# One block instead of two, token sums behind weight pieces, an earlier reciprocal and two warm-up products fewer

## The reference

```python
xn = _layernorm(x)                            # over 512 channels
# attention: 32 query heads, 8 key/value heads, head size 128, window 128
q, k, v = xn @ wq, xn @ wk, xn @ wv
q, k = _rope(q, pos), _rope(k, pos)           # rotary embedding
scores = einsum('bqhgd,bshd->bhgqs', qg, k) * sm_scale     # causal, last 128 positions
s = softmax(scores) @ v @ wo
# feed-forward, inner width 1792, weights = (int - zero) * scale per 128 rows
g = silu(xn @ gate_proj) * (xn @ up_proj) @ down_proj
out = x + s * silu(g)
```

## Time and profile before

| what | value |
|---|---|
| three runs: median (lowest to highest) | 885.1 us (884.85 to 885.5) |
| the profiled execution: its own time | 885.35 us |
| its span, first to last instruction | 883.6 us |
| mean granted TensorE clock | 0.998 of full speed |
| DVE busy | 691.7 us (78%) |
| ACT busy | 485.5 us (55%) |
| POOL busy | 534.6 us (61%) |
| HBM traffic | 69 GB/s over the span |

### The profile page before, as it was taken

The page is one execution under the profiler, slowest core; times in us unless marked ns, Lnnn a source line. Parts: engine busy times, 40 slices in busy tenths (PEclk is TensorE's granted clock), DMA queues, the critical chain, the costliest instruction groups (busy, mean ns, idle before and its releaser), DMA issues. The chain is left out here.

```text
span 883.6 us, 14045 instructions
## 1 busy us (share of the span) xinstructions
PE 870.4 (99%) x4354; PEld 733.2 (83%) x4354; DVE 691.7 (78%) x1106; ACT 485.5 (55%) x1308; POOL 534.6 (61%) x430
## 2 busy tenths in 40 slices
PE   8999999999999999999999999999999999999997
PEld 7778888888888888888888888888877878888886
DVE  7887877877786877877786877877777888889876
ACT  4766556555656565565656565555663334444533
POOL 4675555555555555456555555554457898887865
PEclk9999999999999999999999999999999999999999
DMA  8011010110101011001101010003223464655632
GB/s 255 28 52 37 25 49 24 37 37 29 37 29 36 24 47 36 24 24 36 47 24 36 24 47 24 24 0 108 72 72 108 118 199 147 171 151 155 167 132 96
DMA packets 84596, 61.54 MB, mean 70 GB/s; under 512 B 3664, under 2 KB 71888, under 8 KB 84560
## 3 DMA queue, kind: packets, MB, share of 16 engines
q1 hardware_dynamic: 83840, 59.98, 23.4%
q10 hardware_dynamic: 720, 1.11, 0.3%
HBM read 58.98 MB, written 2.10 MB: 69 GB/s over the span
## 5 line engine op out<-in xcount | busy, mean ns | idle before, releaser
L1333 POOL TENSOR_TENSOR q_lo<-work,q_hi 128x512 fp32r<-128x512 f32 x64 | 82.9, 1295 | 157.8 <-ACT q_hi L1205 157.8
L36 PE MATMUL ps<-xt_hi,w_lo 128*128 128x512 f32 x444 | 175.1, 394 | 1.9 <-PEq L846 1.5
L37 PE MATMUL ps<-xt_lo,w_hi 128*128 128x512 f32 x444 | 173.4, 391 | 0.0
L38 PE MATMUL ps<-xt_hi,w_hi 128*128 128x512 f32 x444 | 173.2, 390 | 0.0
L1338 POOL TENSOR_TENSOR pt_lo<-kept,pt_hi 128x512 fp32r<-128x512 f32 x112 | 143.6, 1300 | 24.5 <-ACT pt_hi L1226 24.5
L1215 ACT ACTIVATE probs<-ps,neg_max 128x128 f32<-128x128 f32 x256 | 90.7, 367 | 53.3 <-DVE neg_max L1484 53.3
L1226 ACT ACTIVATE pt_hi<-kept 128x512 fp32r<-128x512 f32 x112 | 69.2, 633 | 65.7 <-DVE kept L1494 65.7
L36 PE MATMUL ps<-wo_hi,o_lo 128*128 (+1 forms) x256 | 99.8, 390 | 1.1 <-DVE o_lo L1500 1.0
L38 PE MATMUL ps<-wo_hi,o_hi 128*128 (+1 forms) x256 | 99.6, 389 | 0.0
L37 PE MATMUL ps<-wo_lo,o_hi 128*128 (+1 forms) x256 | 99.6, 389 | 0.0
L36 PEld LDWEIGHTS ps<-xt_hi,w_lo 128*128 128x128 f32 x444 | 83.7, 188 | 18.5 <-issue 2.4
(11 more groups left out here) (166 smaller groups left out, 2143.1 us busy)
## 6 DMA issues: line engine op xcount, KB each, us to landing
work<-L_attn_wq SPq DMA_DIRECT2D x32, 256.0 KB, 2.8
work<-L_attn_wo SPq DMA_DIRECT2D x32, 256.0 KB, 2.6
work<-L_ffn_gate_w SPq DMA_DIRECT2D x14, 256.0 KB, 3.4
work<-L_ffn_gate_z SPq DMA_DIRECT2D x14, 256.0 KB, 4.6
work<-L_ffn_gate_s SPq DMA_DIRECT2D x14, 256.0 KB, 5.7
work<-L_ffn_up_w SPq DMA_DIRECT2D x14, 256.0 KB, 3.2
work<-L_ffn_up_z SPq DMA_DIRECT2D x14, 256.0 KB, 3.9
work<-L_ffn_up_s SPq DMA_DIRECT2D x14, 256.0 KB, 4.4
```

Source lines behind the costliest of these rows:

```text
L36: pe.matmul(out, stat[1], mov[0], start=first, stop=False, skip_group_check=grown)
L37: pe.matmul(out, stat[0], mov[1], start=False, stop=False, skip_group_check=grown)
L38: return pe.matmul(out, stat[0], mov[0], start=False, stop=last, skip_group_check=grown)
L1333: pool.tensor_tensor(lo, row_of(unit, b, i), hi.bitcast(F32), ALU.subtract).then_inc(rope_split, 1)
```

## The change

1. Attention and FFN no longer open a block each. Both functions return five lists, and one block runs them one behind the other, so the barrier between is gone. ScalarE gets a wait for the last output projection (`y_ready`) ahead of its first FFN instruction; VectorE had one already.
2. In the last unit GpSimd makes the weight piece first and the x part behind it; `t24` moves from the last attention block to the head of the FFN list. Its `t_lo` parts of the first half stand between or behind the weight pieces 3, 4 and 5.
3. In the first unit, at j = 0 and j = 1, the reciprocal of the next block stands inside the first rotation, between the sine and the cosine products; ScalarE scales before it splits that rotation's result.
4. In the first seven-product block ScalarE's third `copy` stands ahead of the first split of sums for the next block.
5. 22 idle products instead of 24.

```diff
@@ ffn_block, low_parts (GpSimd)
+            sh.t24(pool, 0)
             for n in range(SEVEN_FROM):
                 for e in range(4):
                     ends = n == SEVEN_FROM - 1
                     for at, kind, ii, _ahead in pieces(n, e):
-                        if (n, at) == (0, 5):
-                            sv.t_lo_parts(pool, 0, (T3,))
                         fw.lo(pool, n, at, kind, ii)
+                        if n == 0:
+                            sv.t_lo_parts(pool, 0, {3: (T1,), 4: (T2,), 5: ()}[at])
...
-                    if (n, e) == (0, 1):
-                        sv.t_lo_parts(pool, 0, (T1, T2))
                     if (n, e) == (0, 2):
-                        sv.t_lo_parts(pool, 0, (T4,))
+                        sv.t_lo_parts(pool, 0, (T3, T4))
@@ ffn_block, high_parts (ScalarE)
+            act.wait_ge(sh.y_ready, NKV * TT)
             for n in range(SEVEN_FROM):
...
                 if more:
                     sv.hi_gate(act, blk + 1)
+                if blk == 0:
+                    sv.copy(act, blk, 2)
+                if more:
                     sv.hi_s(act, blk + 1, 0)
-                sv.copy(act, blk, 2)
+                if blk:
+                    sv.copy(act, blk, 2)
@@ attention_block
-        IDLE_PRODUCTS = 24
+        IDLE_PRODUCTS = 22
@@ high_parts (ScalarE), body
+                        early = first_unit(g, b) and j < QB - 1 and left(g, b, j)
+                        if early:
+                            normalise(n + 1)
                         if ahead and j < QB - 1 and left(g, b, j):
                             hi_of_roped(un, bn, left(g, b, j))
...
-                        if more:
+                        if more and not early:
                             normalise(n + 1)
@@ low_parts (GpSimd), body
                         lo_of_probs(unit, j)
-                        if last and b == 1:
-                            pool.wait_ge(scores_ready, UNITS * QB - QB)
-                            if j < QB - 1:
-                                sh.x_part(pool, 0, j)
-                            else:
-                                sh.t24(pool, 0)
...
                         if last:
                             for at in FFN_AT.get((b, j), ()):
                                 fw.lo(pool, 0, at, *fw.piece(at))
+                        if last and b == 1 and j < QB - 1:
+                            pool.wait_ge(scores_ready, UNITS * QB - QB)
+                            sh.x_part(pool, 0, j)
@@ sums (VectorE), rope
+                if between is not None:
+                    invert(between)
                 dve.wait_ge(sin_done, unit * 10 + (2 * i + 2))
                 dve.tensor_tensor(at, at, cos[:, :], ALU.mult).then_inc(cos_done, 1)
@@ build
-        attention_block(nc, sh, fw, x, ...)
-        ffn_block(nc, sh, fw, x, out.rearrange("b s h -> (b s) h"))
+        attention = attention_block(nc, sh, fw, x, ..., sem)
+        ffn = ffn_block(nc, sh, fw, x, out.rearrange("b s h -> (b s) h"), sem)
+        with nc.Block() as block:
+            @block.sync
+            def _(sp):
+                attention[0](sp)
+                ffn[0](sp)
...
```

More of the change, by code:

```diff
@@ L550, in ffn_block @@
         stored = sem("stored")
-        block = ctx.enter_context(nc.Block())
         def place(n, ii, hf):
@@ L560, in pieces, with moves @@
             return [(at, *IN_BODY[at]) for at in BESIDE[e] if n < SEVEN_FROM - 1 or at < 2]
-        @block.sync
-        def _(sp):
+        def moves(sp):
             for n in range(SEVEN_FROM):
@@ L589, in _, with products @@
             sp.wait_ge(stored, 16 * (TT + 1))
-        @block.tensor
-        def _(pe):
+        def products(pe):
             def gate_up(n, e):
@@ L631, in _, with high_parts @@
                 down(PAIRS, TT - 1, True, half, TT - 1 + i)
-        @block.scalar
-        def _(act):
+        def high_parts(act):
             def hi_of_mid(n, ii, hf):
@@ L700, in _, with low_parts @@
                 act.activation(gate_of(TT - 1 + i)[:, half], acc[:, TT - 1, half], ACT.Silu).then_inc(gate_done, 1)
-        @block.gpsimd
-        def _(pool):
+        def low_parts(pool):
             def split_mid(n, ii, hf):
@@ L745, in _, with sums @@
                 pool.tensor_tensor(res[:, t, :], acc[:, t, :], res[:, t, :], ALU.add).then_inc(joined, 1)
-        @block.vector
-        def _(dve):
+        def sums(dve):
             def accumulate(after, t):
@@ L826, in _, with attention_block @@
                 dve.tensor_tensor(res[:, t, half], gate_of(t + i)[:, half], res[:, t, half], ALU.add).then_inc(last_joined, 1)
-def attention_block(nc, sh, fw, x, wq, wk, wv, wo, cos_in, sin_in, causal_in, keep_in, ident_in):
+        return moves, products, high_parts, low_parts, sums
+def attention_block(nc, sh, fw, x, wq, wk, wv, wo, cos_in, sin_in, causal_in, keep_in, ident_in, sem):
     K_, Q_, V_, WO_ = 0, 1, 5, 6
@@ L1457, in rope_first, with rope @@
                 dve.tensor_tensor(direct[:, i % 2, :], at, cos[:, :], ALU.mult).then_inc(proj_drained, 1)
-            def rope(unit, b, i):
+            def rope(unit, b, i, between=None):
                 half, at, to = P // 2, bank(b, i), row_of(unit, b, i)
@@ L1550, in body @@
                             fold_and_max(n + 1, (j + 1) % QB)
+                        early = first_unit(g, b) and j < QB - 1 and left(g, b, j)
                         if ahead and j < QB - 1 and left(g, b, j):
-                            rope(un, bn, left(g, b, j))
+                            rope(un, bn, left(g, b, j), n + 1 if early else None)
                         if ahead and j == QB - 1:
                             lo_of_v(un, bn)
-                        if more:
+                        if more and not early:
                             invert(n + 1)
```

25 lines of the change are left out of this document (20 added, 5 removed).

## The result

The changed kernel takes 880.52 us (median of 5 executions, 880.43 to 880.67), the kernel before 885.1 (5 executions beside it, 884.85 to 886.28): ratio 0.9946, 95% interval 0.9931 to 0.996. That is 4.6 us faster; forecast were 881.1 us and 4.0. The profiled execution took 880.43 us with a span of 878.3, where the one before took 885.35 with 883.6.

The account below looks back on a forecast made before the run. TensorE's own list was taken to bound the kernel, busy 870.4 of 883.6 us. Terms 0 + 0.33 - 1.6 - 1.69 - 1.04 = -4.0 us take 885.35 to 881.35, or 881.1 as a median; range 879.8 to 882.8.

Parts of the forecast that it names:

- Idle products: Start: two fewer gain nothing, as TensorE still waits at 23.76 for VectorE, held by GpSimd; 0 us.
- Early reciprocal: First unit: TensorE's wait at 57.45 goes but returns by 66.77, and VectorE's chain grows; +0.33 us.
- x parts: Last unit: L208 is no longer held twice for 0.8 us by GpSimd, so `o_lo` comes earlier; -1.6 us.
- Barrier: Between attention and FFN: TensorE's stand from 670.60 to 672.45 goes and nothing replaces it at once; -1.69 us.
- what follows it: FFN: GpSimd runs earlier, so TensorE's gaps at 721.75 (-0.33) and 729.29 (-0.71) go; -1.04 us, bounds 0 to -1.1.
- rival (a): FFN: GpSimd binds, its advance staying at its first instruction's 2.65 us; total about -2.8, 882.3 us; chance 0.20 with (b).
- (b): Last unit: x parts don't pay, held time only moves; -0.6 instead of -1.6, 882.1 us; chance 0.20 with (a).
- (c): First unit: the reciprocal pays, its wait not returned at 66.77; -1.5 instead of +0.33, 879.3 us; chance 0.08.
- (d): FFN's start: a wait for ScalarE or a middle stands where the barrier was; 883.5 us; chance 0.07.
- (e): Start: fewer idle products keep TensorE at 1.2 GHz up to the first projections; +15 us, 900 us; chance 0.03.

Follow-up runs that it names:

- the first trace: The changed kernel's first profiled execution, 880.43 us; the second trace is the same kernel run again with no edit, 880.67 us, ratio 0.9944.
- the first group of experiments: First of three groups into which the twelve follow-up runs fall; the kernel before took 885.72 us beside it, median of 9.

## Why the prediction was right

**Idle products, 0 (bounds -0.46 to 0): right, the hold at an earlier place.** 22 and 24 aren't told apart, the wait at 23.8 grew to 0.72 with the weight piece at its old time (0.6 forecast), and the product's time stayed. VectorE gave the head start back near 15.5 already, beside an earlier weight piece of GpSimd, and not at 18.3. The bound's lower end, -0.46, looks like what the first trace shows (-0.47), and would have been taken for it without the second: there it was the DMA. The Trainium skill's page "SBUF — State Buffer", section "Who interferes with whom", has the shared ports as an exclusive lock; this agrees with an instruction of four columns that takes 1.21 us beside one of GpSimd's and 0.16 us without.

**Early reciprocal, +0.33 (bounds -0.1 to +0.6): the mechanism right, the size too large.** The wait went and came back at `o_lo`, `pt_lo` and the transposes of block 3, at the places named, and the chain is longer, but by 0.05 to 0.11 us. I had charged it a wait of 0.12 and its 0.2 at two blocks. The trace shows the reciprocal at 54.70 for 0.18 and the next product at 54.79: the two overlap by half. The wait was as charged (0.83 us from L1464 to the reciprocal, where 0.72 is the distance of two such rows). The reciprocal itself costs 0.09 (start to start), inside the rotation as between two, and not its duration of 0.18.

**x parts, -1.6: -1.66 by the stretches.** The number came from two holds of 0.8 us read off one row against another. The experiment with the x part ahead has the holds, PE's wait and the 1.66 again.

**Barrier, -1.69: -1.62, and what follows it -1.04: -1.18** (-0.11 in the FFN, -1.07 at the seven-product block). I had taken these as two things. They are one account. Going from the old kernel, removing the barrier alone gave 1.62 and kept 1.04 up to the end stage, because GpSimd's list, not TensorE's, ends at the down products; GpSimd's new order (0.99) and the copy (0.75) then give the remaining 1.76, from 207.23 to 205.47 us between the last projection and the end stage. The forecast got this right since it priced GpSimd's advance separately: rival (a), which supposed that the advance stays at the first instruction's, is what the kernel with one block only shows (GpSimd 1.03 us earlier at `mid_lo`, and PE 1.04).

**The sum, -4.0.** By the stretches that repeat it is -4.41: +0.33 was +0.05 (0.28 of it), the other terms were each within 0.14. A term that the prediction did not have, the 0.3 us behind the last transfer's issue, leaves about -4.1. That this is so near to -4.0 is partly luck: too much charged to the reciprocal (0.28) and nothing to the close (0.3) cancel. The rest, to the 4.58 of the medians (5.05 in the first group of experiments), is within the spread of the start and of the loop. The first trace alone has -5.63 on PE, since start and loop both fell well in it.

**Rivals.** (b) fell to the x-part experiment. (c) fell, since the 1.62 us won at j = 1 were gone by 66.78 and the kernel with the early inverse alone has ratio 1.0001. (d) fell: no wait of PE stands where the barrier was. (e) did not happen with 22 products. With 12 the clock did fall, at the transposes and not at the projections, and the start was 0.6 to 1.0 us longer, not 15, since the clock was back in the next stretch.

What the prediction did not have is the loop, whose 0.75 us between two executions of one kernel is a quarter of the forecast's whole range.

## What to carry to other kernels

A barrier's price is what the last engine to reach it still has to do, and what it gives back is limited by the engine that is full behind it: before taking one out, follow that engine's list to the next place where TensorE waits for it, since here 1.04 of the barrier's 1.62 us reached the end stage (and 0.56 the medians) until GpSimd's order was changed too. Put a GpSimd instruction where VectorE reads PSUM or waits, not beside its two-input SBUF work: here moving one kind of 1.3 us instruction behind another gave 1.66 us by the stretches. And subtract traces stretch by stretch between the same two instructions, up to the end of the span, with a second trace of each kernel before a difference below 1 us is given a cause.

## What the runs showed that I had not expected

- One and the same kernel runs its loop of 559 us in one of two times, 559.32 or 558.58, to a hundredth, with the granted clock reading full in both. Its cause is open.
- The third weight piece is taken up 13.57 to 14.39 us after the span's start in the traces with 22 or 24 idle products, and the second transposes of x move with it, from 26.06 to 26.78.
- The stretch from the first 256-column product to the end of the span takes 7.3 us in all kernels with two blocks and 7.5 to 8.1 in those with one. Its cause is open.
- A barrier that all other engines reach before PE costs PE 0.64 us.
- A small reciprocal (0.18 us) delays the next VectorE instruction by 0.09 us only.
- The granted clock halved across a stand of 2.92 us of TensorE at the start (12 idle products), and did not across stands of 0.88 us there or 1.45 us at the barrier.
